# A gated DeltaNet layer on one core: conv taps read PSUM per step, the Gram tile gets a tile of its own, and another order of all engines

## The chip, the core and the metric

The kernel runs on one NeuronCore of one Trainium2 chip. The metric is the time of the whole program on the device in microseconds. The kernel before took 3788.26 us (median of 3 runs, 3783.3 to 3788.53). The engines are TensorE (PE), VectorE (DVE), ScalarE (ACT), GpSimd (POOL) and the sync engine (SP), which here issues all transfers of the loop. All arithmetic is float32.

## The reference

The input is x with 8 batches, 1024 time steps and 128 channels. The first layer, cut to what matters (`x` is layer-normed first, its result layer-normed and added to x; a small gated feed-forward layer of the same shape follows):

```python
def _causal_conv_silu(x, w):                 # 4 taps over time
    xp = jnp.pad(x, ((0, 0), (Kw - 1, 0), (0, 0)))
    y = sum((w[:, j] * xp[:, j:j + x.shape[1], :] for j in range(Kw)))
    return jax.nn.silu(y)
def step(S, inp):                            # over 1024 time steps, 16 heads
    q_t, k_t, v_t, a_t, b_t = inp
    kS = jnp.einsum('bhd,bhdv->bhv', k_t, S)
    kkS = jnp.einsum('bhd,bhv->bhdv', k_t, kS)
    S = a_t[..., None, None] * (S - b_t[..., None, None] * kkS) + jnp.einsum('bhd,bhv->bhdv', k_t, v_t)
    o_t = jnp.einsum('bhdv,bhd->bhv', S, q_t)
    return (S, o_t)
q = _l2_norm(_causal_conv_silu(x @ Wq.T, conv_q))    # 16 heads of 64
k = _l2_norm(_causal_conv_silu(x @ Wk.T, conv_k))    # 16 heads of 64
v = _causal_conv_silu(x @ Wv.T, conv_v)              # 16 heads of 128
alpha = jnp.exp(-jnp.exp(A_log) * jax.nn.softplus(x @ Wa.T + dt_bias))
beta = 2.0 * jax.nn.sigmoid(x @ Wb.T)
o, _S = _gdn_recurrence(q, k, v, alpha, beta)
return _rms_norm(o).reshape(Bx, Tx, H * DV) @ Wo.T
```

## The kernel before

The recurrence is worked in chunks of 64 time steps. A unit of work is a *pair*: two heads (one on each half of the 128 partitions), all 8 batches, and two chunks, called step A and step B. There are 8 head pairs and 8 pairs of chunks, 64 pairs in all, and the state `S` goes from step to step.

For a pair the kernel projects x on k, q and the two halves of v (`pe_proj`, L500, two matmuls of 512 columns for each of the four; a float32 matmul shows as two records in the trace). ScalarE copies the result of two banks to `raw` (`act_raw`, L712), behind a halo of 3 columns, which GpSimd takes from the end of the pair before (`pool_tail`, L1009). ScalarE does tap 0 (`act_tap0`, L720), VectorE taps 1 to 3 (`dve_conv`, L872), all on 1024 columns, and ScalarE the SiLU. Then:

- `gram_k`, `n`: the Gram matrix of k, scaled by decay and beta, goes to `Nd` (L924). `sp_gram` writes it to memory (`scrN`), `sp_gram_in` reads its 16x16 blocks back (`NS`). GpSimd inverts 8x8 blocks by elimination (`pool_elim`, L1060 to L1066) and VectorE joins them (`dve_sub`, L953 to L963).
- The block inverses go out and come back as `Z` and `X0` through `scrZ` and `scrX` (`sp_z_out`, `sp_z_in`, `sp_x_out`, `sp_x_in`). Two rounds of y = N Z, z = X Y (L576, L603) with copies by ScalarE (`act_y`, `act_x`, `act_z1`) and VectorE (`dve_z0`, L973) join them to the inverse of a 64x64 block.
- `vtr`, `ks`, `r`, `u`, `ds`, `s` (L562, L622, L982, L633, L685, L991) do the step of the state; `o1`, `o2` (L643, L646) the output; `ms` its norm; `wo` (L704) the output projection; `yr` and `acc` (L1001, L1088) add it into `accT`.

Each engine has a body written out in a fixed order (`pe_body`, `dve_body`, `act_body`, `pool_body`, `sp_body`), which works at once on several pairs: p0 the newest, p1 the one before it, and so on. The loop runs these bodies 58 times, and ten more are written out ahead of it and behind. An engine does its list strictly in order, and each entry waits on semaphores of its inputs and of those who still read what it overwrites. The table `PB` gives each product its PSUM banks; extra waits in `pe_body` are for banks that are still read. What stands in an engine's list behind a waiting entry waits as well, and this holds for SP, which issues the transfers one after the other. `nc.gpsimd` work on E, QG and `sq` (`diff`, `eb`, `ep`, `qg`, `sq_q`) and ScalarE's `abs`, `exp`, `ln`, `root` make the decay factors and the norms; ScalarE loads another function table four times in a body.

## Time and profile before

| | us |
|---|---|
| median of 3 runs | 3788.26 |
| the profiled execution | 3825.41 |
| its span | 3823.6 |
| TensorE matmul busy | 2960.6 (77%) |
| VectorE busy | 2599.0 (68%) |
| ScalarE busy | 2461.6 (64%) |
| GpSimd busy | 2038.0 (53%) |

The profiled execution took 37 us more than the median. The mean granted clock of TensorE was 0.891 of full speed. Records of neighbouring matmuls overlap, so the step from one to the next is read from the start times. In the timeline a number in brackets is the time the engine stood idle ahead of that group, and behind it stands what ended the wait; "issue" means nothing that the profile shows.

### The profile page before, as it was taken

The numbers are of one execution on the slowest core, as the hardware profiler recorded it, in microseconds if no ns is written. First come the engines' busy times: TensorE is split into PE (matmuls) and PEld (weight loads), VectorE is DVE, ScalarE is ACT, GpSimd is POOL, SyncE is SP. The second block draws the span as 40 slices with busy tenths as digits, with TensorE's granted clock in tenths as the row PEclk, the third lists the DMA queues.
The fourth block names the chain that finished last, engine by engine and source line by source line (L and its number), as shares of the span: only waits on it lengthen the run. The fifth ranks groups of instructions, "written<-read, shape, count | busy, mean of one in ns | idle before, by whom it ended". The sixth has DMA issues, their size and how long they took to land. (4 is left out here: it accounts for less than half of the span.)

```text
span 3823.6 us, 187747 instructions
## 1 busy us (share of the span) xinstructions
PE 2960.6 (77%) x79010; PEld 2359.3 (62%) x79010; DVE 2599.0 (68%) x4634; ACT 2461.6 (64%) x3772; POOL 2038.0 (53%) x2143
## 2 busy tenths in 40 slices
PE   5588887878787877787778788777787878787665
PEld 4366666666666666666666666666666666666533
DVE  5577776767677766676667677666776767776453
ACT  2566666666666666666667666666666667676543
POOL 1356655555555565555555555555555555555335
PEclk9789988999898989898988988989998988889877
DMA  2343433343333334333433343334333433343211
GB/s 64 68 80 71 78 58 76 73 77 58 74 75 76 63 69 80 71 66 66 80 71 67 65 80 71 69 62 79 72 67 64 79 72 67 65 80 71 46 34 44
DMA packets 888600, 262.88 MB, mean 69 GB/s; under 512 B 812992, under 2 KB 862400, under 8 KB 887872
## 3 DMA queue, kind: packets, MB, share of 16 engines
q1 hardware_dynamic: 887584, 250.08, 34.8%
q8 instruction: 704, 11.53, 1.3%
q0 software_dynamic: 288, 1.07, 0.1%
q14 instruction: 24, 0.20, 0.0%
HBM read 177.63 MB, written 56.64 MB: 61 GB/s over the span
## 5 line engine op out<-in xcount | busy, mean ns | idle before, releaser
L872 DVE SCALAR_TENSOR_TENSOR cv<-raw,w_v,cv 128x1024 f32<-128x1024 f32 x384 | 631.6, 1645 | 4.6
L1088 POOL TENSOR_TENSOR accT<-accT,yt 128x512 f32 (+1 forms) x256 | 367.8, 1437 | 462.3 <-DVE yt L1001 459.9
L872 DVE SCALAR_TENSOR_TENSOR cv<-raw,w_kq,cv 128x1024 f32<-128x1024 f32 x384 | 553.9, 1443 | 21.6 <-ACT cv L720 19.3
L982 DVE SCALAR_TENSOR_TENSOR R<-ps,sc,R 128x128 f32<-128x128 f32 x1024 | 281.7, 343 | 318.3 <-PE ps L622 315.6
L712 ACT ACTIVATE raw<-ps 128x1024 f32<-128x1024 f32 x256 | 264.7, 1034 | 277.3 <-PE ps L500 277.3
L973 DVE COPY Z<-ps 16x128 f32<-16x128 f32 x512 | 146.9, 287 | 384.3 <-PE ps L603 378.9
L1075 POOL TENSOR_TENSOR Sg<-S,tabR 128x512 f32<-128x512 f32 x256 | 307.8, 1202 | 164.4 <-DVE S L991 164.4
L1042 POOL TENSOR_TENSOR QG<-sl_q,QG 128x1024 f32<-128x1024 f32 x64 | 166.0, 2594 | 391.5 <-DMA QG<-scrG 391.5
L1009 POOL TENSOR_TENSOR raw<-raw,k_all 128x24 f32<-128x24 f32 x256 | 241.4, 947 | 194.2 <-DVE cv L872 115.2
L576 PE MATMUL ps<-Z,Nd 64*64 64x64 f32 x8192 | 204.1, 242 | 172.9 <-DMA Z<-scrZ 164.5
L500 PE MATMUL ps<-xnT,w_kq 128*128 (+1 forms) x512 | 322.1, 785 | 13.4 <-DMA w_kq<-wtab 13.4
L802 ACT ACTIVATE R<-ps,sc 128x128 f32<-128x128 f32 x1024 | 278.6, 383 | 78.3 <-PE ps L562 75.8
L704 PE MATMUL ps<-wo_s,oo 128*128 128x128 f32 x2048 | 301.9, 299 | 0.0
L813 ACT ACTIVATE XY<-ps 128x512 f32<-128x512 f32 x256 | 151.8, 593 | 225.7 <-PE ps L576 223.1
L576 PEld LDWEIGHTS ps<-Z,Nd 64*64 64x64 f32 x8192 | 179.3, 155 | 187.7 <-issue 187.6
L643 PE MATMUL ps<-QG,S 64*64 64x64 f32 x8192 | 247.9, 221 | 59.5 <-issue 59.3
L1026 POOL TENSOR_TENSOR Nd<-E,sc 128x512 f32<-128x512 f32 x128 | 133.4, 1042 | 291.3 <-ACT E L763 235.3
L840 ACT ACTIVATE U<-ps 128x512 f32<-128x512 f32 x256 | 152.9, 597 | 208.9 <-PE ps L633 208.8
L633 PE MATMUL ps<-R,Z 64*64 64x128 f32 x4096 | 276.4, 274 | 6.2 <-issue 6.2
L622 PE MATMUL ps<-S,kB 64*64 64x128 f32 x2048 | 115.8, 392 | 207.3 <-issue 207.2
L704 PEld LDWEIGHTS ps<-wo_s,oo 128*128 128x128 f32 x2048 | 262.7, 204 | 14.0 <-issue 0.2
L500 PE MATMUL ps<-xnT,w_v 128*128 (+1 forms) x512 | 266.3, 643 | 2.6 <-DVE sc L918 2.1
(198 smaller groups left out, 7687.1 us busy)
## 6 DMA issues: line engine op xcount, KB each, us to landing
E<-scrE SPq DMA_DIRECT2D x128, 256.0 KB, 4.7
scrN<-Nd SPq DMA_DIRECT2D x256, 128.0 KB
Z<-scrZ SPq DMA_DIRECT2D x128, 256.0 KB, 5.6
X<-scrX SPq DMA_DIRECT2D x512, 64.0 KB
QG<-scrG SPq DMA_DIRECT2D x128, 256.0 KB, 4.1
kB<-sk SPq DMA_DIRECT2D x64, 256.0 KB
w_kq<-wtab SPq DMA_DIRECT2D x64, 132.0 KB, 3.4
w_v<-wtab SPq DMA_DIRECT2D x64, 132.0 KB, 3.1
```

Of the source, the lines that this page charges most:

```text
L500: last = nc.tensor.matmul(bank(PB["P" + "kqvw"[j]] + g), w[:, (j % 2) * P:(j % 2 + 1) * P], xnV[:, 4 * g:4 * g + 4, bass.ds((p % 8) * P, P ...
L576: last = nc.tensor.matmul(ps[place(cls, a), col64(PB["y1" if l else "y0"][s], cls, i)], blk(Nd, s, b, a), blk(Z, s, b, a), start=True, sto ...
L633: last = nc.tensor.matmul(ps[a:z, col128(PB["u"][s], g, i)], blk(Z, s, b, a), unit(R, b)[a:z], start=True, stop=True)
L643: last = nc.tensor.matmul(ps[d:d + 64, o:o + C], S[a:z, b * P + d:b * P + d + 64], blk(QG, s, b, a), start=(b == 0), stop=False)
L704: last = nc.tensor.matmul(ps[:, col128(PB["wo"][s], h, i)], oo[:, h * 512 + i * P:h * 512 + (i + 1) * P], wo_s[:, h * D:(h + 1) * D], star ...
L712: nc.scalar.activation(raw3[j][:, :, HALO:HALO + P], b3(bank(PB["P" + "kqvw"[j]], 2)), ACT.Copy).then_inc(raw_ok[j].sem, 1)
L802: last = nc.scalar.activation(unit(R, b), ps[:, col128(PB["vt"][s], h, i)], ACT.Copy, scale=rv[:, 8 * s + b:8 * s + b + 1])
L872: nc.vector.scalar_tensor_tensor(cv3[j], raw3[j][:, :, k:k + P], tap(j, k), cv3[j], ALU.mult, ALU.add).then_inc(conv[j].sem, 1)
L982: last = nc.vector.scalar_tensor_tensor(unit(R, b), ps[:, col128(PB["ks"][s], g, i)], cr[:, 8 * s + b:8 * s + b + 1], unit(R, b), ALU.mult ...
L1009: nc.gpsimd.tensor_tensor(raw3[j][:, :, 0:HALO], raw3[j][:, :, P:P + HALO], tails[:, bass.ds(p, 1)].rearrange("p (o u) -> p o u", u=1).to_ ...
L1075: nc.gpsimd.tensor_tensor(half(Sg, g).rearrange("p (b v) -> p b v", b=4), half(S, g).rearrange("p (b v) -> p b v", b=4), gam, ALU.mult).th ...
L1088: nc.gpsimd.tensor_tensor(dst, dst, row(half(yt, h)), ALU.add).then_inc(acc_ok[h][s].sem, 1)
```

## The change

- A projection is done for one step at a time: two matmuls of 4 x 67 columns (64 steps and the halo of 3 ahead of them, read from x itself, whose columns ahead of time 0 are zeros). There are eight per pair instead of four. Tap 0 and taps 1 to 3 read this product in PSUM directly, on 512 columns each: 8 and 24 operations instead of 4 and 12. The tile `raw`, its copy (`act_raw`) and `pool_tail` are gone.
- `pe_y` reads the Gram tile from a new tile `NM`, which SP loads from `scrN` (`sp_nm`, two transfers of 256 KB). GpSimd's write of the next `Nd` no longer waits for the last y.
- `z0`, the copy of the first product of the inverse, moves from VectorE to ScalarE.
- All five bodies have another order, and `PB` other banks. A body now works on three pairs (p0 to p2) instead of four; the loop runs 59 times, with eight bodies written out.

```diff
-        PB = {"Pk": 0, "Pq": 4, "Pv": 0, "Pw": 4, "nk": 4, "nq": 6, "gk": [4, 0], "gp": [4, 2], "ktr": [6, 4], "vt": [2, 4], "y0": [0, 2], "z0": [0, 6], "y1": [6, 6], "xt": [0, 4], "z1": [6, 0], "ks": [2, 2], "u": [2, 2], "ds": [2, 6], "o": [6, 6], "ms": [6, 4], "wo": [0, 2]}
+        PB = {"Pk": [2, 6], "Pq": [2, 6], "Pv": [2, 0], "Pw": [6, 4], "nk": 6, "nq": 4, "gk": [4, 6], "gp": [0, 4], "ktr": [4, 4], "vt": [6, 0], "y0": [0, 2], "z0": [0, 4], "y1": [6, 6], "xt": [0, 0], "z1": [4, 4], "ks": [2, 6], "u": [2, 4], "ds": [6, 6], "o": [2, 0], "ms": [2, 4], "wo": [4, 4]}
...
-        def pe_proj(pe, p, j):
+        def pj(j, s):
+
+            return bank(PB["P" + "kqvw"[j]][s], 2).rearrange("p (b t) -> p b t", b=NB)
+
+        def pe_proj(pe, p, s, j):
             w_in = (wkq_in, wv_in)[j // 2]
             pe.wait_ge(w_in.sem, w_in.at(p))
             pe.sem_inc(pe_go.sem, 1)
             w = (w_kq, w_v)[j // 2]
             for g in range(2):
-                last = nc.tensor.matmul(bank(PB["P" + "kqvw"[j]] + g), w[:, (j % 2) * P:(j % 2 + 1) * P],
-                                        xnV[:, 4 * g:4 * g + 4, bass.ds((p % 8) * P, P)], start=True, stop=True)
-            last.then_inc(proj[j].sem, 1)
+                last = nc.tensor.matmul(pj(j, s)[:, 4 * g:4 * g + 4, 0:CW], w[:, (j % 2) * P:(j % 2 + 1) * P],
+                                        xnT3[:, 4 * g:4 * g + 4, bass.ds((p % 8) * P + s * C, CW)], start=True, stop=True)
+            last.then_inc(proj[j][s].sem, 1)
...
-                pe.wait_ge(nd_ok[s].sem, nd_ok[s].at(p))
+                pe.wait_ge(nm_in.sem, nm_in.at(p))
...
-                        last = nc.tensor.matmul(ps[place(cls, a), col64(PB["y1" if l else "y0"][s], cls, i)], blk(Nd, s, b, a),
+                        last = nc.tensor.matmul(ps[place(cls, a), col64(PB["y1" if l else "y0"][s], cls, i)], blk(NM, s, b, a),
...
-        def act_raw(act, p, j):
-            act.wait_ge(proj[j].sem, proj[j].at(p))
-            act.wait_ge(tail[j].sem, tail[j].at(p))
-            nc.scalar.activation(raw3[j][:, :, HALO:HALO + P], b3(bank(PB["P" + "kqvw"[j]], 2)), ACT.Copy).then_inc(raw_ok[j].sem, 1)
-
-        def act_tap0(act, p, j):
-            act.wait_ge(raw_ok[j].sem, raw_ok[j].at(p))
+        def act_tap0(act, p, s, j):
+            act.wait_ge(proj[j][s].sem, proj[j][s].at(p))
             if j >= 2:
                 act.wait_ge(silu[j - 2].sem, silu[j - 2].at(p))
             elif not first(p):
                 act.wait_ge(silu[j + 2].sem, silu[j + 2].at(p - 1))
-            nc.scalar.activation(cv3[j], raw3[j][:, :, 0:P], ACT.Copy, scale=tap(j, 0)).then_inc(tap0[j].sem, 1)
+            nc.scalar.activation(cv3[j][:, :, s * C:(s + 1) * C], pj(j, s)[:, :, 0:C], ACT.Copy, scale=tap(j, 0)).then_inc(tap0[j][s].sem, 1)
...
+        def act_z0(act, p, s):
+
+            act.wait_ge(z_mm[0][s].sem, z_mm[0][s].at(p))
+            zp = quads(PB["z0"][s]).rearrange("p g (b c) -> p g b c", b=4)
+            zs = two(half(Z, s)).rearrange("p g (b c) -> p g b c", b=4)
+            for r in range(0, P, 32):
+                o = r % C
+                last = nc.scalar.activation(zs[r:r + 16, :, :, o + 16:o + 32], zp[r:r + 16, :, :, o + 16:o + 32], ACT.Copy)
+            last.then_inc(z_ok[0][s].sem, 1)
...
-        def dve_conv(dve, p, j, k):
+        def dve_conv(dve, p, s, j, k):
             if k == 1:
-                dve.wait_ge(tap0[j].sem, tap0[j].at(p))
+                dve.wait_ge(tap0[j][s].sem, tap0[j][s].at(p))
             else:
-                dve.wait_ge(conv[j].sem, conv[j].at(p, k - 1))
-            nc.vector.scalar_tensor_tensor(cv3[j], raw3[j][:, :, k:k + P], tap(j, k), cv3[j],
-                                           ALU.mult, ALU.add).then_inc(conv[j].sem, 1)
+                dve.wait_ge(conv[j][s].sem, conv[j][s].at(p, k - 1))
+            c = cv3[j][:, :, s * C:(s + 1) * C]
+            nc.vector.scalar_tensor_tensor(c, pj(j, s)[:, :, k:k + C], tap(j, k), c, ALU.mult, ALU.add).then_inc(conv[j][s].sem, 1)
...
-        def pool_tail(pool, p, j):
-            if not first(p):
-                pool.wait_ge(conv[j].sem, conv[j].at(p - 1))
-            pool.sem_inc(pool_go.sem, 1)
-            nc.gpsimd.tensor_tensor(raw3[j][:, :, 0:HALO], raw3[j][:, :, P:P + HALO],
-                                    tails[:, bass.ds(p, 1)].rearrange("p (o u) -> p o u", u=1).to_broadcast([P, NB, HALO]),
-                                    ALU.mult).then_inc(tail[j].sem, 1)
...
-                pool.wait_ge(y_mm[1][s].sem, y_mm[1][s].at(p - 1))
...
+                sp.wait_ge(nm_in.sem, nm_in.at(p - 1))
...
+        def sp_nm(sp, p):
+            if not first(p):
+                sp.wait_ge(y_mm[1][B].sem, y_mm[1][B].at(p - 1))
+            sp.sem_inc(sp_go.sem, 1)
+            sp.wait_ge(n_out.sem, n_out.at(p))
+            for h, (a, z) in enumerate(HALF):
+                sp.dma_start(NM[a:z].rearrange("p (n t) -> p n t", t=C), rows(scrN, h)).then_inc(nm_in.sem, 16)
...
```

(`+                sp.wait_ge(nm_in...)` stands in `sp_gram`, `- pool.wait_ge(y_mm...)` in `pool_eb`. `act_yr` and `pool_sq_k`, new functions, are not in the bodies.)

The order on the engines at three places inside the loop body, first before, then after. `x16` counts equal instructions; rows named ISA and REGISTER_ALU set registers.

TensorE from ds(B) (before) and wo(A) (after) to the first product with the inverse, y(A,0), which is L576 before and L573 after:

```order
L685 MATMUL ps<-U,KT 64x128 x16
L500 MATMUL ps<-xnT,w_v 128x512 x2
L553 MATMUL ps<-k_all,sk 64x64 x16
L622 MATMUL ps<-S,sk 64x128 x16
L570 ISA
L576 MATMUL ps<-Z,Nd 64x64 x16
L522 MATMUL ps<-k_all,sq 64x64 x32
```

```order
L701 MATMUL ps<-wo_s,oo 128x128 x8
L619 MATMUL ps<-S,sk 64x128 x16
L550 MATMUL ps<-k_all,sk 64x64 x16
L1301 REGISTER_ALU
L497 MATMUL ps<-xnT,w_kq 128x4x67 x2
L566 ISA
L573 MATMUL ps<-Z,NM 64x64 x16
L519 MATMUL ps<-k_all,sq 64x64 x32
```

Ahead of y stand now ks and ktr in the other order and a projection (L497) between; y reads `NM`. At the top of the body stand now two projections with z(B,1) (L600) between them, where before it was ks(B) and the projections of q and k.

VectorE around the four operations of `sub` (L953 to L963 before, L971 to L981 after):

```order
L982 SCALAR_TENSOR_TENSOR R<-ps,sc,R 128x128 x4
L872 SCALAR_TENSOR_TENSOR cv<-raw,w_v,cv 128x1024
L918 TENSOR_TENSOR sc<-ps,sc 128x8
L951 ISA
L952 ISA
L953 TENSOR_TENSOR tmpS<-NS,XT 128x512
L956 ISA
L958 TENSOR_REDUCE tmpW<-tmpS 128x8x8
L956 REGISTER_ALU
L960 TENSOR_TENSOR tmpS<-XT,tmpW 128x512
L956 REGISTER_ALU
L963 TENSOR_REDUCE XT<-tmpS 128x8x8
```

```order
L1000 SCALAR_TENSOR_TENSOR R<-ps,sc,R 128x128 x8
L936 TENSOR_TENSOR sc<-ps,sc 128x8
L969 ISA
L970 ISA
L971 TENSOR_TENSOR tmpS<-NS,XT 128x512
L974 ISA
L976 TENSOR_REDUCE tmpW<-tmpS 128x8x8
L974 REGISTER_ALU
L978 TENSOR_TENSOR tmpS<-XT,tmpW 128x512
L974 REGISTER_ALU
L981 TENSOR_REDUCE XT<-tmpS 128x8x8
L1685 REGISTER_ALU
```

`sub` stood behind the taps of v and r(B), some ten entries into the body, and worked on the pair p1; it is now the last entry of the body and works on p0, whose Gram tile was made in that same body.

SP at the top of its body:

```order
L1100 DMA w_kq<-wtab 128x264
L1144 ISA
L1146 ISA
L1147 ISA
L1148 DMA NS<-scrN 128x16x16
L1151 ISA
L1153 ISA
L1154 DMA scrZ<-XT 128x16x16
L1107 ISA
L1107 DMA w_v<-wtab 128x264
```

```order
L1116 DMA w_kq<-wtab 128x264
L1150 ISA
L1151 DMA kB<-sk 128x512
L1172 ISA
L1174 DMA NM<-scrN 64x16x64 x2
L1177 ISA
L1179 ISA
L1180 DMA scrZ<-XT 128x16x16
L1186 ISA
L1187 DMA scrX<-XB 128x16x16
L1190 ISA
L1195 DMA Z<-scrZ 64x16x64 x2
```

The load of `kB` and the two loads of `NM` stand now ahead of the stores to `scrZ` and `scrX`, the load of `NS` has gone to the end of the body, and the load of `Z` comes right behind the stores.

## Rows read from the trace of the kernel before

**Rows 1.** The page, part 1: busy time, share of the span, instructions.

```profile
PE 2960.6 (77%) x79010; PEld 2359.3 (62%) x79010; DVE 2599.0 (68%) x4634; ACT 2461.6 (64%) x3772; POOL 2038.0 (53%) x2143
```

**Rows 2.** One line, 1000 to 3000 us: duration ns min/median/max, first and last start.

```profile
L763 ACT ACTIVATE E<-E x37: 1056/1057/1058, 1029.4 to 2993.5; 128x1024 f32<-128x1024 f32 x37
```

**Rows 3.** Busy time of each engine in a window of the loop.

```profile
1000.00:2000.00 1000.00, 796.19 (x22395) 638.86 (x22394) 700.14 (x1124) 669.44 (x1031) 558.83 (x583) 0.91 0.39 71
```

**Rows 4.** Waits of PE, 1000 to 3000 us: total, times, longest.

```profile
PE ps L622 <- issue: 130.9, 37, 4.1
PE ps L576 <- DMA Z<-scrZ: 97.4, 37, 3.3
PE ps L553 <- issue: 46.3, 31, 2.5
PE ps L511 <- issue: 45.7, 28, 4.0
PE ps L643 <- issue: 33.9, 35, 1.8
PE ps L603 <- issue: 22.7, 41, 1.1
```

**Rows 5.** Timeline of PE in one pass: start, us, line, count, idle before.

```profile
1985.23 2.05 PE L704 MATMUL ps<-wo_s,oo 128*128 128x128 f32 x16
...
1997.51 0.84 PE L576 MATMUL ps<-Z,Nd 64*64 64x64 f32 x32 [2.41 <-DMA Z<-scrZ]
...
2001.96 0.60 PE L553 MATMUL ps<-k_all,sk 64*64 64x64 f32 x12 [1.47 <-issue]
...
2009.64 1.98 PE L500 MATMUL ps<-xnT,w_v 128*128 x4
...
2012.18 1.16 PE L704 MATMUL ps<-wo_s,oo 128*128 128x128 f32 x8
...
2026.67 1.99 PE L622 MATMUL ps<-S,kB 64*64 64x128 f32 x32 [3.54 <-issue]
2028.58 5.41 PE L500 MATMUL ps<-xnT,w_kq 128*128 x8
```

**Rows 6.** Busy time in a window behind the load of Z; PEclk follows POOL.

```profile
2000.00:2002.00 2.00, 0.53 (x24) 0.45 (x17) 0.00 (x0) 0.28 (x1) 0.00 (x0) 0.50 0.64 185
```

**Rows 7.** Taps and PSUM operations: page part 5, then single lines, 1000 to 3000 us.

```profile
L872 DVE SCALAR_TENSOR_TENSOR cv<-raw,w_v,cv 128x1024 f32<-128x1024 f32 x384 | 631.6, 1645 | 4.6
...
L872 DVE SCALAR_TENSOR_TENSOR cv<-raw,w_kq,cv 128x1024 f32<-128x1024 f32 x384 | 553.9, 1443 | 21.6 <-ACT cv L720 19.3
...
L872 DVE SCALAR_TENSOR_TENSOR cv<-raw,w_kq,cv x222: 1232/1283/3389, 1006.1 to 2991.3; 128x1024 f32<-128x1024 f32 x111
...
L991 DVE TENSOR_TENSOR S<-ps,Sg x146: 674/681/693, 1010.7 to 2974.0; 128x512 f32<-128x512 f32 x146
...
L982 DVE SCALAR_TENSOR_TENSOR R<-ps,sc,R x584: 332/342/353, 1014.2 to 2978.8; 128x128 f32<-128x128 f32 x195
```

**Rows 8.** The page, part 5: copies and tails; busy us, mean ns, idle before.

```profile
L712 ACT ACTIVATE raw<-ps 128x1024 f32<-128x1024 f32 x256 | 264.7, 1034 | 277.3 <-PE ps L500 277.3
L973 DVE COPY Z<-ps 16x128 f32<-16x128 f32 x512 | 146.9, 287 | 384.3 <-PE ps L603 378.9
...
L1009 POOL TENSOR_TENSOR raw<-raw,k_all 128x24 f32<-128x24 f32 x256 | 241.4, 947 | 194.2 <-DVE cv L872 115.2
...
L813 ACT ACTIVATE XY<-ps 128x512 f32<-128x512 f32 x256 | 151.8, 593 | 225.7 <-PE ps L576 223.1
```

**Rows 9.** Timeline of SP: the issue of the Z loads.

```profile
1989.65 1.34 SPq L1169 DMA_DIRECT2D Z<-scrZ  x2
```

**Rows 10.** Timeline of DVE and POOL: end of n(B), start and end of the elimination.

```profile
2015.91 0.69 DVE L924 TENSOR_TENSOR Nd<-ps,Nd 128x512 f32<-128x512 f32 x1 [0.77 <-PE ps L533]
...
2026.34 0.20 POOL L1060 COPY XT<-NS 128x14 f32<-128x14 f32 x1 [2.77 <-DMA NS<-scrN]
...
2032.46 2.36 POOL L1031 TENSOR_TENSOR E<-E,k_all 128x1024 f32<-128x1024 f32 x1
```

775 lines of the change are left out of this document (354 added, 421 removed).

## The prediction

> **What bounds the kernel now.** I read the page's first part, then the time of one pass of the pair loop, then the busy time in a window inside the loop, then who waits on TensorE, and last the timeline of one pass. The page shows no full engine: TensorE 77%, VectorE 68%, ScalarE 64%, GpSimd 53% [rows 1]. The loop shows its period in one instruction that runs once per pair: 37 starts from 1029.4 to 2993.5 us, so 1964.1 / 36 = 54.56 us [rows 2]. 64 of them are 3492 us of the 3823.6, so this number decides. In a window of 1000 us TensorE is busy for 796 us, that is 43.4 of 54.56 us; VectorE 38.2, ScalarE 36.5, GpSimd 30.5 [rows 3]. TensorE is the fullest, and what it does not work is 11.1 us per pair.
>
> The waits of TensorE over 2000 us, which are 36.7 pairs [rows 4], say where. 130.9 us, 3.57 per pair, stand ahead of the first matmul of the loop body (L622) and have no releaser: this is the return of the loop. 97.4 us, 2.65 per pair, are waits of the first product with the inverse (L576) for the load of Z. 148.6 us (L553, L511, L643 and L603 together), 4.05 per pair, are "issue" again, inside the body; one of them lies in the middle of a group of 32 equal matmuls [rows 5], where no semaphore is waited for. The rest, 0.8, is small. The stretches behind the waits are slow as well: behind the Z load the granted clock is 0.50 (1.2 GHz) [rows 6], and behind the loop's return the eight records of two projections take 5.41 us where four take 1.98 at full clock [rows 5]. Over the window the clock is 0.91, so (1 - 0.91) x 2 x 54.56 = 9.8 us per pair are at half clock, and cost 4.9 us.
>
> **What the change removes.** Four copies of a projection to `raw` on ScalarE, 4 x 1.034 = 4.1 us per pair, and four small GpSimd operations on the tails, 4 x 0.94 = 3.8 us [rows 8]. Eight copies of 16 partitions (`z0`) leave VectorE, 8 x 0.287 = 2.3 us [rows 8], and go to ScalarE, where their price is not in the trace. They read PSUM like the 512-column copy that takes 0.593 [rows 8], so 8 x 0.287 = 2.3 to 8 x 0.593 = 4.7; I take 2.3, as they are small. Neither ScalarE (36.5 of 54.56) nor GpSimd (30.5) is full, so the sums alone save nothing. ScalarE ends near 36.5 - 4.1 + 2.3 = 34.7. What hides it is TensorE, and if that cover went, ScalarE would come next to VectorE.
>
> **What the taps cost in the new form.** Before: 12 per pair over 1024 columns from `raw`, mean (631.6 + 553.9) / 768 = 1.544 us, 18.5 per pair, though the fastest takes 1.232 [rows 7]. After: 24 over 512 columns from PSUM, which no row shows as such. Lower bound: the PSUM operation of 512 columns, 0.681, with every one of 146 of them between 0.674 and 0.693 [rows 7]. Upper bound: no gain from the halved size, 1.283 (median of the 1024 columns). The same operation on 128 columns from PSUM takes 0.342; with 384 more columns at the slope to the 1024-column one, (1.283 - 0.342) / 896 = 1.05 ns a column, it is 0.745, and I take that: 24 x 0.745 = 17.9. VectorE goes from 38.2 to 38.2 - 18.5 - 2.3 + 17.9 = 35.3. The bounds give 33.7 and 48.2.
>
> The spread of these rows bears on a rule. The 1024-column tap has a longest time of 3.389 against a fastest of 1.232, the PSUM operation no spread at all [rows 7]. The Trainium skill (SBUF — State Buffer, "SBUF: two separate sides") says that a VectorE operation with two SBUF inputs and a GpSimd operation lock each other out for whole instructions; by that rule, the trace agrees, the new taps have one SBUF input and keep their price. Against the change speaks the Trainium skill, VectorE: DVE Perf Modes ("Rules for kernel authors" and "The TRN2 errata"): copy PSUM to SBUF first if many operations read it, since the fixed part is 120 cycles from PSUM and 58 from SBUF. By its figures at 0.96 GHz the estimate is 24 x 0.658 = 15.8 us after and 12 x 1.127 = 13.5 before, a loss of 2.3 on VectorE; the trace has 1.544 for the old tap and not 1.127, and so the loss isn't there.
>
> **What TensorE gets.** Eight projections per pair of 2 x 268 columns (64 steps plus a halo of 3, per step) instead of four of 2 x 512. The step between records is 1.98 / 4 = 0.495 at 512 columns and 1.16 / 8 = 0.145 at 128 [rows 5]; on the line between, 268 columns are 0.273. 32 x 0.273 = 8.7 against 16 x 0.495 = 7.9: **+0.8 us** per pair. The rows on either side bound it: at 0.145 a record -3.3, at 0.495 +7.9; 268 columns lie nearer to the 128 ones, and the line between is what I take.
>
> **The Z wait.** Before, TensorE comes to y(A,0) soon after its last wait, and the two Z loads, issued at 1989.65, let it go at 1997.51, 7.9 us later [rows 5, 9]. After, the Z loads stand behind `x_out`, which waits for ScalarE's `xb`. From the start of TensorE's body: u(B,1) ends at 6.4, ScalarE copies it (0.6) and does `xb` (0.65 in this pass), so 7.8; Z is issued at 8.3 and there at 16.2. On TensorE stand ahead of y(A,0): two half-size projections and a z at half clock 4.6, two u 1.8, o1 with gram_p and o2 2.9, a projection 1.1, ds 1.05, ms 1.2, two vtr 1.1, two wo 2.05 [rows 5], ks and ktr 2.0, a projection 1.1: 18.9 us (those without a row here are read from this same pass). It comes 2.7 us after the load: **-2.65 us**, with 0 and -2.65 as bounds. The two NM loads, new, are issued ahead of Z, once the last y has read the old NM; by the same 7.9 us they are there some 10 us before their use.
>
> **The clock.** With the Z wait goes the cause of one of the two slow stretches; the one behind the loop's return stays, with 6 to 8 us. From 9.8 us at half clock to 6.2: **-1.8 us**; bounds 0 (the issue wait behind y keeps it) and -3.
>
> **The loop's return.** The NM loads, 512 KB in 256-byte rows, are issued when the last y ends, and run just while TensorE returns to the top of the body. Mean 3.57 with 4.1 at most before [rows 4] where little moves. I take **+0.5**, from 0 to +2.5 (another wait like L553's maximum).
>
> **New waits.** Projections now wait for banks that taps still read (`conv` of step A or B). I laid the body out with the durations above. VectorE's first three taps of step A are ready at 7.2, TensorE asks at 9.4; k's second step 8.7 against 10.4; q's A 15.3 against 15.8; v1's A 36.8 against 37.8; v1's B 38.2 against 38.9. All in time, by 0.5 to 2 us. The inverse's chain closes inside a body now: n(B) ends at 30.2, the elimination starts 9.7 us later (2016.6 to 2026.34, [rows 10]), takes 6.1 and `sub` 4.3: 50.3, while VectorE's first tap of the next body is due at 51.4 + 4.2. **+0.2** for handovers that have no slack (x, y(B,1), z(A,1)); bounds 0 and +4.
>
> **Sum.** 54.56 + 0.8 - 2.65 - 1.8 + 0.5 + 0.2 = 51.6 us per pair, 3.0 less; 64 x 3.0 = 190 us. Own time of the profiled execution 3825.4, so 3635 for such a one. The median of the runs is 37 lower (3788.3), so **3600 us**. The parts ahead of and behind the loop do not change by more than a few us: a last body that only adds to accT (some 1.3 us of GpSimd) goes.
>
> **Rivals.**
> (1) *The body packs tighter.* The 4.05 us of issue waits inside the body are partly answers to bursts after a wait; if half goes with the Z wait, and the clock gives 3, the period is 51.6 - 2.0 - 1.2 = 48.4 and the time 3788 - 64 x 6.2 = 3391; with a third of the extra 3.2, 3530. For it: nothing else in the layout asks TensorE to wait. Against: the waits lie within groups, and the number of instructions rises.
> (2) *The gain is half eaten.* The return of the loop grows by 1.5 instead of 0.5 under the NM loads, or the clock stays: period 51.6 + 1.0 to 1.8, time 3665 to 3715. For it: one issue wait in the middle of a group follows on the loads of X, kB and QG. Against: 4.1 at most.
> (3) *Slower: VectorE becomes the bound.* It decides in the taps. At 1.283 each VectorE has 48.2 us of work; it also stands idle for the first 4.2 us of a body (the first tap needs a projection and tap0) and 2.0 for ds ahead of S, so 54.4, and each tap that then holds a bank is a wait of TensorE: period 55.2, time 3788 + 64 x 0.6 = 3826. The point from which it decides is 1.26 us per tap. Against: 512 columns from PSUM took 0.693 at most.
> (4) *Nothing happens*: the Z wait goes over into a wait for X or NM of the same size, and the clock stays; period 54.4 to 54.7, 3780 to 3795.
>
> **Chances.** Forecast 50% (3560 to 3640), (1) 17% (below 3560), (2) 19% (3640 to 3780), (4) 3%, (3) 11%. The range 3510 to 3740 leaves out the far half of (1), some 6%, and (3), (4) and the last of (2), some 15%. Within 0.2% is 3781 to 3796, about what a measurement of this kernel can tell from no change. Faster 86%, same 3%, slower 11%.
>
> **What would show it.** Period 51.6 in the starts of Exp on E. No TensorE wait for Z over 0.5 us per pair; 3.6 to 4.5 at the first matmul of the body; taps at 0.745 with little spread; granted clock 0.94 in the loop; L1009 and the copies to `raw` gone. Wrong if the taps are over 1 us, if a wait of TensorE for VectorE's taps or for NM heads the list, or if the return of the loop takes over 6 us.

## The result and the profile after: slower by 3%

The changed kernel took 3903.26 us (median of 4 runs, 3878.92 to 3910.84) against 3787.52 for the kernel before (4 runs): a ratio of 1.0297, 95% interval 1.025 to 1.0343. The forecast was 3600. The profiled execution took 3906.49 us.

The page and the main rows of the changed kernel, against [rows 1], [rows 7] and [rows 8]:

```profile
PE 3080.1 (79%) x80034; PEld 2508.7 (64%) x80034; DVE 2396.3 (61%) x4890; ACT 2422.7 (62%) x4280; POOL 1568.2 (40%) x1886
...
L891 DVE SCALAR_TENSOR_TENSOR cv<-ps,w_kq,cv 128x512 f32<-128x512 f32 x768 | 557.9, 747 | 431.1 <-ACT cv L712 419.7
...
L497 PE MATMUL ps<-xnT,w_kq 128*128 (+1 forms) x1024 | 403.1, 529 | 233.0 <-issue 219.6
...
L497 PE MATMUL ps<-xnT,w_v 128*128 (+1 forms) x1024 | 327.6, 445 | 1.4 <-DVE cv L891 1.4
...
L825 ACT ACTIVATE Z<-ps 16x128 f32<-16x128 f32 x512 | 137.9, 269 | 169.6 <-PE ps L600 165.1
...
NM<-scrN SPq DMA_DIRECT2D x128, 256.0 KB, 4.7
```

VectorE and ScalarE have less to do than before, as forecast (the tap takes 0.747, the copy z0 0.269), and TensorE is busy 120 us longer. The same line as [rows 2] gives the period, 1911.3 / 34 = 56.21 us, where the forecast was 51.6:

```profile
L758 ACT ACTIVATE E<-E x35: 1057/1058/1060, 1033.5 to 2944.8; 128x1024 f32<-128x1024 f32 x35
```

The window from 1000 to 3000 us, that is 35.58 pairs (columns as in [rows 3]: busy us of PE, PEld, DVE, ACT, POOL, then clock, DMA share, GB/s):

```profile
1000.00:3000.00 2000.00, 1615.39 (x43675) 1323.59 (x43671) 1253.30 (x2309) 1275.32 (x2270) 811.54 (x984) 0.93 0.40 78
```

TensorE is busy 45.4 us per pair. Its waits over the same 2000 us, which answer to [rows 4]:

```profile
PE ps L497 <- issue: 135.5, 36, 4.2
PE ps L519 <- issue: 53.0, 35, 3.2
PE ps L682 <- issue: 49.6, 35, 2.0
PE ps L643 <- issue: 43.5, 36, 1.6
PE ps L619 <- issue: 31.8, 68, 1.1
PE ps L519 <- DVE KT L955: 26.0, 26, 1.2
PE ps L583 <- ACT Z L825: 12.2, 35, 0.4
PE ps L530 <- ACT XY L808: 11.6, 35, 0.3
```

The wait for the load of Z is gone. The waits "issue" stand at four lines in nearly every pass, beside the return of the loop (L497, 3.81 per pair). With the smaller rows that are not shown, "issue" adds up to 330.7 us and the waits with a name to 49.8; for the kernel before, in the same window, to 293.3 and 109.2, with 1596.33 busy. Per pair:

| us per pair | before | after | difference | forecast |
|---|---|---|---|---|
| TensorE busy | 43.5 | 45.4 | +1.9 | -1.0 (projections +0.8, clock -1.8) |
| "issue", the loop's return with it | 8.0 | 9.3 | +1.3 | +0.5 |
| waits with a name | 3.0 | 1.4 | -1.6 | -2.45 (Z -2.65, new waits +0.2) |
| period | 54.56 | 56.21 | +1.65 | -2.95 |

The column "before" comes from the profiled execution of [rows 1], which took 37 us more than its median, 0.6 us per pair.

Three groups in the timeline of one pass of the changed kernel (columns as in [rows 5]):

```profile
2014.85 2.15 PE L497 MATMUL ps<-xnT,w_kq 128*128 x4 [3.98 <-issue]
...
2023.12 0.51 PE L643 MATMUL ps<-PT,U 64*64 64x64 f32 x19
2024.96 0.45 PE L643 MATMUL ps<-PT,U 64*64 64x64 f32 x13 [1.33 <-issue]
2025.35 1.18 PE L497 MATMUL ps<-xnT,w_kq 128*128 x4
...
2033.35 1.18 PE L497 MATMUL ps<-xnT,w_kq 128*128 x4
2034.46 0.69 PE L573 MATMUL ps<-Z,NM 64*64 64x64 f32 x32
2036.09 0.81 PE L519 MATMUL ps<-k_all,sq 64*64 64x64 f32 x39 [0.94 <-DVE KT L955]
2037.82 0.58 PE L519 MATMUL ps<-k_all,sq 64*64 64x64 f32 x25 [0.93 <-issue]
2038.33 2.00 PE L497 MATMUL ps<-xnT,w_v 128*128 x4
```

y(A,0) (L573) starts 19.6 us after the body does, where the layout had 18.9, and waits for nothing: this part of the forecast held. But a group of 32 equal matmul records is cut after 19 and waits 1.33 us, and one of 64 is cut after 39. No semaphore stands there. What follows can be slow as well. Behind the first stop the granted clock stays at 1.00 (2024 to 2026 us) and the projection at 2025.35 takes 1.18 us. The second stop comes right after the wait for KT; from 2038.3 to 2040.3 us the clock is 0.56, near its lower level (1.2 GHz), and the projection at 2038.33 takes 2.00. Of the 287 projections whose four records lie together in the window, 81 took more than 1.5 us.

### The profile page after: what moved, and what is told of

Same layout as the page of the kernel before. It is cut to its first block and busy times, and to the rows that moved or that the text cites. A ratio compares the mean times of both kernels' runs of the same rounds, so it can differ in the third digit from the quotient of the medians.

```text
span 3904.5 us, 191127 instructions
## 1 busy us (share of the span) xinstructions
PE 3080.1 (79%) x80034; PEld 2508.7 (64%) x80034; DVE 2396.3 (61%) x4890; ACT 2422.7 (62%) x4280; POOL 1568.2 (40%) x1886
## 5 line engine op out<-in xcount | busy, mean ns | idle before, releaser
L891 DVE SCALAR_TENSOR_TENSOR cv<-ps,w_kq,cv 128x512 f32<-128x512 f32 x768 | 557.9, 747 | 431.1 <-ACT cv L712 419.7
L891 DVE SCALAR_TENSOR_TENSOR cv<-ps,w_v,cv 128x512 f32<-128x512 f32 x768 | 552.4, 747 | 81.8 <-ACT cv L712 73.4
L497 PE MATMUL ps<-xnT,w_kq 128*128 (+1 forms) x1024 | 403.1, 529 | 233.0 <-issue 219.6
L497 PEld LDWEIGHTS ps<-xnT,w_kq 128*128 128x128 f32 x1024 | 229.1, 248 | 294.9 <-issue 242.0
L1009 DVE TENSOR_TENSOR S<-ps,Sg 128x512 f32<-128x512 f32 x256 | 165.0, 686 | 307.3 <-PE ps L682 307.3
L497 PE MATMUL ps<-xnT,w_v 128*128 (+1 forms) x1024 | 327.6, 445 | 1.4 <-DVE cv L891 1.4
L862 ACT ACTIVATE osq<-ps 128x1024 f32<-128x1024 f32 x128 | 131.2, 1025 | 302.5 <-PE ps L643 302.5
L643 PE MATMUL ps<-PT,U 64*64 64x64 f32 x8192 | 242.5, 220 | 78.8 <-issue 78.5
L701 PE MATMUL ps<-wo_s,oo 128*128 128x128 f32 x2048 | 282.7, 288 | 2.0 <-ACT oo L854 1.4
L1019 DVE TENSOR_TENSOR yt<-ps,sc 128x512 f32<-128x512 f32 x256 | 170.7, 687 | 179.8 <-PE ps L701 172.0
L643 PEld LDWEIGHTS ps<-PT,U 64*64 64x64 f32 x8192 | 208.4, 135 | 87.5 <-issue 87.5
L630 PEld LDWEIGHTS ps<-R,Z 64*64 64x64 f32 x4096 | 225.9, 135 | 57.2 <-issue 57.1
L701 PEld LDWEIGHTS ps<-wo_s,oo 128*128 128x128 f32 x2048 | 252.9, 198 | 12.1 <-issue 2.3
L825 ACT ACTIVATE Z<-ps 16x128 f32<-16x128 f32 x512 | 137.9, 269 | 169.6 <-PE ps L600 165.1
```

The lines of the kernel that those rows point to most:

```text
L497: last = nc.tensor.matmul(pj(j, s)[:, 4 * g:4 * g + 4, 0:CW], w[:, (j % 2) * P:(j % 2 + 1) * P], xnT3[:, 4 * g:4 * g + 4, bass.ds((p % 8) ...
L630: last = nc.tensor.matmul(ps[a:z, col128(PB["u"][s], g, i)], blk(Z, s, b, a), unit(R, b)[a:z], start=True, stop=True)
L643: last = nc.tensor.matmul(ps[d:d + 64, o:o + C], U[a:z, b * P + d:b * P + d + 64], blk(PT, s, b, a), start=False, stop=(b == NB - 1))
L701: last = nc.tensor.matmul(ps[:, col128(PB["wo"][s], h, i)], oo[:, h * 512 + i * P:h * 512 + (i + 1) * P], wo_s[:, h * D:(h + 1) * D], star ...
L825: last = nc.scalar.activation(zs[r:r + 16, :, :, o + 16:o + 32], zp[r:r + 16, :, :, o + 16:o + 32], ACT.Copy)
L891: nc.vector.scalar_tensor_tensor(c, pj(j, s)[:, :, k:k + C], tap(j, k), c, ALU.mult, ALU.add).then_inc(conv[j][s].sem, 1)
```

## The theory, and the experiments

A stop inside a group of equal instructions is no matter of data. The transfers have a queue of their own for instructions (page part 3; then the same rows of a window from 2022 to 2024 us of that pass; columns: packets, MB, share of 16 engines):

```profile
q8 instruction: 707, 11.58, 1.3%
...
q8 instruction: 1, 0.02, 3.8%
```

That is 16.4 KB a packet, 11 packets per pair. Of the 16 windows of 2 us from 2010 to 2042, six hold one packet; the two stops above end at 2024.96 and 2037.82, and the windows of 2022 and 2034 hold one each, 1.0 to 3.8 us earlier. The queue serves all engines, so a single packet cannot be put down to TensorE. Over the whole window the two go together: TensorE has 165 "issue" waits of more than 0.6 us there, and every one of them ends between 1.2 and 2.3 us after a packet has landed (median 1.45), while a moment taken at random lies 2.6 us behind the last packet in the median. In the kernel before it is 131 such waits with a median of 1.50, of which one in twenty comes over 3 us behind. **Theory C**: TensorE's program comes in blocks, and with 64 matmul records in 1.1 us it reaches the end of a block before the next is there; the loop's return is such a load as well. What a body costs then depends on where in it the block borders fall. **The rival** is that the parts of the change cost what was measured: the halved projections, the taps, the NM loads.

The Trainium skill (Runtime: NRT & Kernel Launch, "Instruction fetch mechanics") says that an engine's program is refilled in blocks of 16 KiB, 256 instructions, that a border is "mostly hidden", and that a branch taken out of the window forces a load. The packet size agrees, and so does the stop at the loop's return; "mostly hidden" does not: there are 5.5 us per pair of such stops inside the body.

### All bodies written out, no loop (e1, e2)

```diff
-            for i in range(5):
-                body(eng, *at(i))
-            with eng.Fori(2, PAIRS - 3) as j:
-                body(eng, j + 3, j + 2, j + 1, j)
-            for i in range(PAIRS, PAIRS + 3):
+            for i in range(PAIRS + 3):
                 body(eng, *at(i))
```

The same in the kernel before, with its own bounds (68 bodies). Expected, first of the changed kernel, then of the one before:

> The changed kernel with all 67 bodies written out one after the other instead of a loop. Theory A: TensorE bounds the pair, and its 3.84 us wait at the first matmul of the loop body (135.5 us in 35.3 pairs) is the price of the return of the loop, so it goes: 59 x 3.84 = 227 us, plus some 1 us per pair of half clock behind it; 3903 goes to 3620 to 3690. Theory B: the wait only covers work of the other engines (the last y, its copy by ScalarE, the last sub of VectorE), so it turns into named waits and the time falls by less than 100 us.

> The kernel before with all 67 bodies written out. Theory A: 58 x 3.57 = 207 us and about 1 us per pair of half clock less: 3788 goes to 3510 to 3590. If theory A holds in both kernels, the gap between them stays at 90 to 140 us, since the loop's return isn't what sets them apart. If the NM loads made the return dearer, as I had forecast, the gap falls by 59 x 0.27 = 16 us.

Measured: the changed kernel 3523.97 us (3509 to 3531; ratio 0.930, 0.9251 to 0.935), the kernel before 3659.59 (ratio 0.9659, 0.9616 to 0.9703). Written out, the changed kernel is 136 us **faster** than the kernel before. Both expectations missed: the changed kernel gained more than either theory gave it (3620 was the lowest), the kernel before less (3590 was the highest), and the gap was expected to stay at 90 to 140 us the other way round. The changed kernel's period and its waits:

```profile
L758 ACT ACTIVATE E<-E x41: 1056/1057/1059, 1007.2 to 2998.5; 128x1024 f32<-128x1024 f32 x41
```

```profile
PE ps L643 <- issue: 34.9, 24, 2.5
PE ps L519 <- issue: 32.1, 18, 2.5
PE ps L640 <- issue: 30.4, 19, 2.8
PE ps L540 <- issue: 28.6, 17, 2.6
PE ps L600 <- issue: 22.5, 22, 1.8
```

The period is 49.78 us. The return has gone, and the stops no longer stand at fixed lines: each line has one in about half the passes, as the borders fall elsewhere in each copy of the body. All "issue" comes to 5.9 us per pair instead of 9.3. In the kernel before, written out, it is 5.9 as well (of 8.0), but these stand at the head of its list:

```profile
PE ps L576 <- DMA Z<-scrZ: 86.4, 38, 4.0
PE ps L562 <- DVE PT L931: 46.5, 24, 3.3
```

The Z wait stays, and a wait for PT has come. So unrolled, the gain that the forecast saw in the waits is there: those with a name are 4.2 before and 0.7 after. TensorE's busy time is not lower, though, but higher: 43.1 us per pair against 41.6.

### The program moved by idle instructions (e8 to e13, e17)

```diff
                 pe.wait_ge(g_cp.sem, g_cp.at(0))
+                for _k in range(128):
+                    pe.sem_inc(pe_go.sem, 1)
                 program(pe, pe_body)
```

128 here and in e12 and e17; 64 in e9 and e11; 192 in e10 and e13. They run once, ahead of all bodies.

> The changed kernel with 128 semaphore increments, which do nothing, ahead of the pair bodies on TensorE (some 2 to 8 us in all), so that its program lies 128 instructions further on. Theory C (the issue waits are loads of program blocks of 16 KB, 256 instructions of 64 B): the waits inside the body move from ds (L682), o2 (L643), ks (L619) and nq (L519) to other lines, and the wait at the top of the body changes, because its target lies elsewhere in its block; the time changes by up to 100 us either way. Theory D (they belong to the operations, as a hidden dependency): same lines, same sizes, 3903 plus 2 to 8 us.

> The changed kernel with 64 idle semaphore increments ahead of TensorE's pair bodies. At 128 of them it took 3830 against 3903. Theory C (the place of the program in its 256-instruction blocks sets the waits): again other lines, and a time between 3810 and 3920. Theory D' (any delay ahead of the loop helps): near 3830 as with 128.

> The changed kernel with 192 idle increments. Theory C: between 3810 and 3920, with the waits in other lines than at 0, 64 and 128.

> The kernel before with 64 idle increments ahead of TensorE's pair bodies. Theory C: its time moves too, though less, since the wait for Z and others take up what the block waits leave: 3770 to 3830. If the kernel before has a lucky place in its blocks (theory L), most shifts make it slower, up to 3850, and the mean over the places of both kernels lies within 30 us. If only the changed kernel depends on the place, it stays within 10 us of 3788.

> The kernel before with 128 idle increments: as for 64, 3770 to 3830 by theory C, up to 3850 by theory L.

> The kernel before with 192 idle semaphore increments ahead of TensorE's loop bodies; nothing in the bodies changes. At shifts of 0, 64 and 128 the kernel before took 3788, 3993 and 3910 us, so its position in the instruction memory is worth 205 us, and this run completes the four quarter positions of a 256-instruction block. Theory L (the kernel before stands at a lucky position, the changed one at an average one): this position is slower than 3788 too, 3860 to 3990, and the mean of the four positions of before is 3890 or more, equal to or above the changed kernel's mean of 3905. Rival W (the changed kernel is slower by its own work at any position; before has two good and two bad ones): 3780 to 3820, mean of before 3870, below the changed one's by 35 us or more.

Measured; the last four columns of each kernel are per pair, from the window 1000 to 3000 us of each run's trace, as above:

| idle | before, us | period | busy | issue | named | after, us | period | busy | issue | named |
|---|---|---|---|---|---|---|---|---|---|---|
| 0 | 3788 | 54.6 | 43.5 | 8.0 | 3.0 | 3903 | 56.2 | 45.4 | 9.3 | 1.4 |
| 64 | 3993 | 57.2 | 43.7 | 11.9 | 1.5 | 3958 | 57.4 | 45.2 | 11.3 | 0.8 |
| 128 | 3910 | 55.6 | 43.1 | 10.6 | 1.9 | 3830 | 54.4 | 44.9 | 8.7 | 0.5 |
| 192 | 3922 | 55.6 | 43.8 | 8.3 | 3.4 | 3930 | 56.2 | 44.7 | 10.6 | 0.8 |
| mean | 3903 | 55.7 | 43.5 | 9.7 | 2.5 | 3905 | 56.1 | 45.1 | 10.0 | 0.9 |

Sixty-four instructions that do nothing cost the kernel before 205 us (ratio 1.0544, 1.0477 to 1.061); 128 of them make the changed kernel 73 us faster (ratio to before 1.0119, 1.0098 to 1.014). The expectations for e9 to e12 were all too low (at most 3920 and 3850): the position moves the time by more than theory C had given it. That 64 of them are slower and 128 faster in the changed kernel rules out that any delay ahead of the loop helps (theory D'). For the last position of the kernel before, 3860 to 3990 us were expected if it was luck and 3780 to 3820 if not; 3922 came. Over the four positions the two kernels are equal as far as four positions can tell: they spread over 205 and 128 us, so the means are uncertain by some tens of us. At its own position the kernel before is 115 us under its mean, and the changed one 2 us under its own. So the 116 us of the result are, in the main, the luck of the position that the kernel before had.

The instruction queue shows the shift as well. Only TensorE's program moved, and the kernel before with 64 idle instructions fetched 58 packets more than its 704, one for each of its 58 loop passes:

```profile
q8 instruction: 762, 12.48, 1.4%
```

With 128 it is 762 too, with 192 it is 705; the changed kernel goes from 707 to 765 in all three. Written out, the two fetch 634 and 644, about one packet per pass less than with the loop. The number does not order the times (3830 us with 765 packets, 3922 with 705), so it is where the borders fall and not how many there are. With 128 idle instructions two of the four largest stops of the changed kernel stand at lines that had none (L693, L701), and those at L519 and L682 are gone:

```profile
PE ps L497 <- issue: 157.1, 36, 4.7
PE ps L643 <- issue: 45.5, 48, 1.5
PE ps L693 <- issue: 44.0, 55, 1.3
PE ps L701 <- issue: 27.9, 33, 2.0
```

And in the kernel before with 64 of them, three lines have risen against [rows 4] or are new there, while the Z wait is cut to 53.0:

```profile
PE ps L622 <- issue: 183.2, 35, 5.6
PE ps L522 <- issue: 74.3, 34, 2.5
PE ps L576 <- issue: 67.9, 66, 2.0
PE ps L576 <- DMA Z<-scrZ: 53.0, 35, 4.6
```

So a wait that goes need not be a gain of its size: stops and the Z wait seem to stand in for each other, since the load of Z goes on while TensorE stands at a border. The rows fit that without proving it: over the positions of the kernel before, "issue" moves by 3.9 us per pair and its sum with the named waits by 2.4 (11.0, 13.4, 12.5, 11.8).

The control, the shift of 128 in the unrolled changed kernel:

> The changed kernel with all bodies written out (3524 us) and 128 idle semaphore increments ahead of TensorE's bodies. Theory L: what the position decides is where the block borders fall in the body that is repeated 62 times; written out, 67 bodies have their borders at different places, so the shift does next to nothing: 3505 to 3545. Rival (the unrolled times too are one draw out of a wide spread, and the 136 us between the two unrolled kernels say little): off 3524 by 50 us or more to either side.

Measured: 3535.76 us (3525 to 3549; ratio 0.9348, 0.9315 to 0.9382), where e1 had 0.930. As expected by theory L, the shift does nothing that is sure there, so the 3524 us of the changed kernel do not hang on the position. The unrolled kernel before was not shifted by itself; e14 below moves its program by other instructions and takes 3666 us where it took 3660.

### The halved projections (e3, e14)

```diff
-            for g in range(2):
-                last = nc.tensor.matmul(bank(PB["P" + "kqvw"[j]] + g), w[:, (j % 2) * P:(j % 2 + 1) * P],
-                                        xnV[:, 4 * g:4 * g + 4, bass.ds((p % 8) * P, P)], start=True, stop=True)
+            for s in range(2):
+                for g in range(2):
+                    last = nc.tensor.matmul(b3(bank(PB["P" + "kqvw"[j]], 2))[:, 4 * g:4 * g + 4, s * C:(s + 1) * C],
+                                            w[:, (j % 2) * P:(j % 2 + 1) * P],
+                                            xnV[:, 4 * g:4 * g + 4, bass.ds((p % 8) * P + s * C, C)], start=True, stop=True)
```

In the kernel before (e3) and in the unrolled one (e14):

> The kernel before, only each projection is done in four matmuls of 256 columns (one per step and half of the batches) instead of two of 512, with the same results in the same places. Theory A (TensorE's own work and instruction stream bound the pair, and the halved projections are what it lost): 1.2 to 2.4 us per pair more, so 3865 to 3940 against 3788. Theory B (the other order and the handovers cost the time, not the halved projections): less than 30 us more.

> The kernel before with all bodies written out (3660 us) and, alone, each projection issued as four matmuls of 256 columns in place of two of 512. In the looped kernel the same split cost 103 us, but it also moved every block border of TensorE's program. Theory L (most of that was position): the work alone is 8 x 1.0 (four records of about 0.265) against 4 x 1.93 us per pair, so 0.3 to 1.0 us per pair, 20 to 65 us: 3680 to 3725. Rival W (the split itself costs it, by more instructions and more block loads): 90 us or more: 3750 and up.

With the loop it took 3891.39 us (ratio 1.027, 1.0224 to 1.0316). That is as much as theory A had said and alone looks like the whole of the result, which would have been wrong: unrolled it took 3666.30 (ratio 0.9658, 0.962 to 0.9696) against 3659.59 (0.9659), nothing that is sure, and less than either expectation. In the loop it had also moved the block borders. A row of e14 shows two split projections side by side:

```profile
2008.58 3.72 PE L501 MATMUL ps<-xnT,w_kq 128*128 128x256 f32 x16
```

That is 0.93 us for four records of 256 columns, 0.97 for 268. In the changed kernel four records stand alone between other groups, and the step to the next group is 1.11 (2033.35 to 2034.46). Against a row of halved projections, 8 x (1.11 - 0.97) = 1.1 us per pair are the price of standing alone, and 8 x 0.04 = 0.3 that of the halo. Counted over the window of the traces, with each overlap of two groups given to the earlier one, the projections take 7.7 us per pair in the unrolled kernel before, 7.9 in e14 and 9.3 in the unrolled changed kernel. So it is the projections that make TensorE busier there (43.1 against 41.6), by their place, the halo and the time at half clock that falls on them (1.0 us per pair against 0.4), and not by being halved.

### The taps (e4, e15)

```diff
-            nc.scalar.activation(cv3[j][:, :, s * C:(s + 1) * C], pj(j, s)[:, :, 0:C], ACT.Copy, scale=tap(j, 0)).then_inc(tap0[j][s].sem, 1)
+            nc.scalar.activation(rj(j, s), pj(j, s)[:, :, 0:CW], ACT.Copy).then_inc(raw_ok[j][s].sem, 1)
+            act.wait_ge(raw_ok[j][s].sem, raw_ok[j][s].at(p))
+            nc.scalar.activation(cv3[j][:, :, s * C:(s + 1) * C], rj(j, s)[:, :, 0:C], ACT.Copy, scale=tap(j, 0)).then_inc(tap0[j][s].sem, 1)
...
-            nc.vector.scalar_tensor_tensor(c, pj(j, s)[:, :, k:k + C], tap(j, k), c, ALU.mult, ALU.add).then_inc(conv[j][s].sem, 1)
+            nc.vector.scalar_tensor_tensor(c, rj(j, s)[:, :, k:k + C], tap(j, k), c, ALU.mult, ALU.add).then_inc(conv[j][s].sem, 1)
```

In the changed kernel (e4), and unrolled (e15). TensorE's program is the same, so no border moves.

> The changed kernel with the on-chip copy back: ScalarE copies each half-size projection (67 columns per batch) to a tile in SBUF, and all four taps read that tile. The order of all engines stays. Theory A: TensorE bounds and the other engines have slack, so eight more copies of 0.65 us on ScalarE and slower taps on VectorE (two inputs in SBUF) cost less than 1.5 us per pair: 3903 to 4000. Theory B (ScalarE and VectorE chains bound): the copies lie in the chain to each tap, at least 5 us per pair more, 4200 or higher.

> The changed kernel with all bodies written out (3524 us) and, alone, the copy of each projection step to on-chip memory put back on ScalarE, with tap0 and the taps reading the copy. In the looped kernel the same edit cost 261 us with TensorE's program unchanged. Theory T (the taps on PSUM are a real gain of the change, since VectorE's taps from on-chip memory are slow beside GpSimd, and ScalarE's chain grows by 8 copies): 90 to 260 us slower here as well, 3615 to 3785. Rival P (it was the loop that made it so dear: a late ScalarE moved TensorE's stalls): under 60 us, 3584 at most.

Measured: 4164.09 us (ratio 1.0975, 1.0916 to 1.1033), 261 more than the changed kernel, and unrolled 3860.81 (ratio 1.017, 1.013 to 1.0209), 337 more than e1. With the loop this lies between the two theories (at most 4000, at least 4200), unrolled above both. The taps of e15, and the same line of the changed kernel:

```profile
L899 DVE SCALAR_TENSOR_TENSOR cv<-rw,w_v,cv 128x512 f32<-128x512 f32 x437 | 475.9, 1124 | 34.1 <-ACT cv L720 30.1
L899 DVE SCALAR_TENSOR_TENSOR cv<-rw,w_kq,cv 128x512 f32<-128x512 f32 x438 | 403.5, 943 | 110.5 <-ACT cv L720 103.9
...
L899 DVE SCALAR_TENSOR_TENSOR cv<-rw,w_kq,cv x438: 740/752/2898, 1015.7 to 2997.5; 128x512 f32<-128x512 f32 x146
```

```profile
L891 DVE SCALAR_TENSOR_TENSOR cv<-ps,w_kq,cv x432: 741/750/752, 1010.0 to 2997.8; 128x512 f32<-128x512 f32 x144
```

The medians are equal, 0.752 and 0.750, but from on-chip memory the longest is 2.898 and the mean about 1.0, from PSUM the longest is 0.752. The copies on ScalarE come on top (8 of 0.609 in e4). In e15 TensorE then waits for taps:

```profile
PE ps L565 <- DVE cv L899: 66.5, 36, 2.2
```

It waits for `sc` of VectorE as well (21.3 us) and for U and XY of ScalarE (44.6 and 20.2), so both engines hold it up. Beside eight copies of a half projection, reading PSUM is a gain of 260 us or more in this order; how much of it is the taps and how much ScalarE's copies was not separated, and the four larger copies of the kernel before were not tried against it. The Trainium skill (SBUF — State Buffer, "SBUF: two separate sides") has a VectorE operation with two SBUF inputs and a GpSimd operation that reads SBUF lock each other out; the spread of these rows agrees with it.

### z0 on ScalarE (e16)

```diff
+                dve_z0(dve, p1, A)
...
-                act_z0(act, p1, A)
```

The same for step B. The first line stands in `dve_body`, the second in `act_body`.

> The changed kernel with all bodies written out (3524 us) and, alone, the 16-partition copies of z back on VectorE. ScalarE loses 2.2 us per pair and VectorE gains 2.3. Theory Q (neither engine sets the end, TensorE's own queue does): 3510 to 3545. Rival (the place of the copy in VectorE's order holds y back, VectorE being late behind the taps): 3560 to 3620.

Measured: 3607.45 us (ratio 0.9515, 0.9472 to 0.9559), 83 more than e1: the rival holds.

```profile
PE ps L583 <- DVE Z L991: 52.8, 40, 2.4
```

The copy costs nearly the same on either engine, but on VectorE it stands behind taps and TensorE waits for it, 1.3 us per pair where it waits 0.3 for ScalarE (10.7 us in e1). Moving it is a gain by its place in the queue, not by its price.

### The NM loads (e7, e18)

```diff
-        def sp_nm(sp, p):
...
-            for h, (a, z) in enumerate(HALF):
-                sp.dma_start(NM[a:z].rearrange("p (n t) -> p n t", t=C), rows(scrN, h)).then_inc(nm_in.sem, 16)
+        def pool_nm(pool, p):
...
+            nc.gpsimd.tensor_copy(NM[:], Nd[:]).then_inc(nm_in.sem, 1)
```

> The changed kernel with NM filled by a GpSimd copy from Nd (it stands first in GpSimd's body, where that engine is idle for 24 us) instead of the two loads from memory; 512 KB of transfers less per pair. My forecast had 0.5 us per pair for these loads at the return of the loop: then 20 to 45 us less. Theory A (return and block loads don't depend on the data queue): within 15 us of 3903, and the wait at the first matmul stays at 3.8 us.

> The changed kernel with all bodies written out (3524 us) and NM copied by GpSimd from Nd in place of the two loads back from memory. Candidate for the best version. Theory: the NM loads delay nothing that TensorE waits for, and GpSimd has room (40% busy): 3505 to 3535, as the looped kernel gained 10 us. Rival: the copy on GpSimd, 0.5 us or more, locks VectorE's taps or comes late behind nd: 3550 and up.

Measured: with the loop 3893.28 us (ratio 1.028, 1.0257 to 1.0303), and the wait at the return is

```profile
PE ps L497 <- issue: 133.1, 36, 4.0
```

as against 135.5. So theory A holds, and the loads do not lengthen the return, which the forecast's +0.5 had assumed. Unrolled, 3483.40 us (3478 to 3498; ratio 0.9214, 0.9189 to 0.9239), against 0.9348 for e17 on the same chip. This is better than its theory had it (3505 at least), and **the best version**: 8% under the kernel before and 11% under the changed one. Its clock was 0.963 and its period 49.22; the rows do not say by which way the 0.6 us per pair come. The copy takes 1.40 us on GpSimd.

### Half of the products of q's norm left out (e5, e6)

```diff
-            for s in range(2):
+            for s in range(1):
```

One step of `pe_nq`, 16 of its 32 matmuls per pair (32 records), is left out, so that the norms of q for step B aren't computed. This removes work of TensorE and moves its borders.

> The changed kernel without the norms of q of step B (16 of the 32 matmuls of nq are left out, so the output norms of step B are wrong). Nothing waits for less than before but TensorE's own work shrinks by 32 records of 64 columns and 32 weight loads. Theory A (TensorE's work and instruction stream are the period): 0.9 us of work and, with 64 of some 2560 instructions, 0.1 to 0.3 us of the waits inside the body: 1.0 to 1.3 us per pair, 64 to 83 us, 3903 to 3820 to 3840. Theory B (handovers bound, in which TensorE only seems to wait for nothing): under 15 us.

> The kernel before without the norms of q of step B, as in the run on the changed kernel. It stands right behind the product that waits for Z. The unrolled version gained only 2.1 us per pair where its return wait was 3.6, so a second limit lies close under TensorE here. Theory A': 0.3 to 0.9 us per pair, 20 to 58 us less. If TensorE alone bounded it, 64 to 83 us less; if the Z chain alone, under 10 us.

Measured: the changed kernel 3762.40 us (ratio 0.9923, 0.9896 to 0.995), 141 less; the kernel before 3798.63 (ratio 1.0034, 1.0014 to 1.0054), 11 more. Neither expectation held (64 to 83 us less for the first, 20 to 58 less for the second). Less work made one kernel faster by more than the work and the other slower. In e5 the stops stood elsewhere again:

```profile
PE ps L497 <- issue: 150.3, 37, 4.3
PE ps L643 <- issue: 54.1, 37, 1.8
PE ps L600 <- issue: 52.6, 62, 1.5
PE ps L550 <- issue: 38.1, 37, 1.4
```

L519 and L682, which head the list of the changed kernel behind the return, are no longer among these; L600 and L550 are new. Both results fit the position and not the work alone.

## Why the prediction was wrong, point by point

Two steps failed: the terms for TensorE's busy time, which make up most of the miss, and the "issue" waits, which were carried over as a constant. Per pair the period came out 4.6 us above the forecast (56.21 against 51.6): 2.9 of it is busy time (+1.9 for -1.0), 0.8 is "issue" (+1.3 for +0.5) and 0.85 waits with a name.

- **The "issue" waits inside the body.** The forecast read the 4.05 us per pair as a constant and carried them over without a cause. It had seen that one lay "in the middle of a group of 32 equal matmuls", and drew nothing from it. In the same window all "issue" outside the return was 4.4 before and 5.5 after, and the return 3.6 and 3.8; over four positions "issue" with the return goes from 8.0 to 11.9. The forecast compared a kernel at a good position with one at a position unknown. On the runs' means the luck is 115 of the 303 us between forecast and result.
- **The mean over the positions.** The other 188 us are about the whole gain that was forecast, and it did not come at the mean of the positions either: -3.0 us per pair was forecast and +0.3 came (55.7 to 56.1). Named waits went down by 1.6, less than the 2.45 of the forecast, and TensorE's busy time went up by 1.5 where 1.0 less was forecast.
- **The projections**, +0.8, are a term of the sum that was mis-sized. The rows of L497 add up to 730.7 us for the run, 11.4 per pair, against (322.1 + 266.3) / 64 = 9.2 before. With overlaps given to the earlier group they take 9.0 us per pair of the window before and 10.9 after, +2.0. The record step on the line between was right (1.11 / 4 = 0.278 against 0.273), so at full clock the difference is 8 x 1.11 - 7.9 = 1.0. The other 1.0 is half clock, which the forecast had counted elsewhere and as a gain: of the projections' time 3.0 us per pair lay at half clock before and 4.3 after.
- **The Z wait** went as forecast, and the layout held to 0.7 us up to y(A,0). But a new wait for KT (0.73) and two small ones for ScalarE (0.67 together) came, against +0.2 for new waits.
- **The clock** rose as forecast, from 0.90 to 0.93 in the window (1000 to 2000 us before: 0.91). By the forecast's own way of counting that is (0.10 x 54.56) - (0.07 x 56.21) = 1.5 us of the 1.8. But the gain did not arrive. What TensorE does outside the projections is busy 34.6 us per pair before and 34.5 after, although its part at half clock fell from 6.1 to 2.3. So what it does at full clock has grown; which groups pay that, and whether it is the many changes between short groups, no run shows. Unrolled it is the same: 34.0 and 33.7 us outside the projections, of which 4.7 and 1.5 at half clock.
- **The taps** (0.745 forecast, 0.747 measured), z0 (2.3 and 2.2 us per pair), VectorE (35.3 and 35.2) and ScalarE (34.7 and 35.8) were right. They are far from the bound. What the taps are worth showed only when the copies were put back: 261 and 337 us.
- **The return of the loop**, 3.81 us, lies in the 3.6 to 4.5 that was named, but not for the reason given: the NM loads don't touch it (e7).
- **The rivals.** The slower case named VectorE as the bound, from 1.26 us a tap; it did not come about. Rival (1) had the stops as answers to a wait, to go with it; they did not go (4.4 and 5.5 us per pair inside the body). No case had the position of the program in it, nor busy time that does not fall with the clock, and so 11% for slower was too little.

What is still open: why a given border costs 0.9 in one place and 2.5 us in another, why TensorE's work outside the projections grew, what share of the taps' gain is ScalarE's, and what the new order of the bodies is worth, which no run tried by itself.

## What to carry to other kernels

A wait without a releaser in the middle of a group of equal instructions, or at the top of a loop body, was a load of the program here: in the changed kernel each one over 0.6 us ended 1.2 to 2.3 us behind a packet of the instruction queue. A busy time is not the engine's work alone, since the granted clock is in it; check which groups a change moves into the slow stretches. In a looped kernel that is full of short matmuls, its sum depends on where the program lies, here by 205 us in 3900 for 64 idle instructions, so a change of a few per cent is judged over several positions or with the loop written out, and one position of an edit proves nothing. Write the loop out first where it fits: it was worth 128 to 379 us here, more than the change itself, and only then did the removed wait show as a gain.
